# Fused cross-attention and routed feed-forward: last quad and tail reordered, one weight load of the first quad a step later

## The chip, the cores and the metric

The kernel runs on one core of a Trainium2 chip. The metric is device time in microseconds (us). The engines are TensorE (PE, matrix products; PEld is its weight load), VectorE (DVE), ScalarE (ACT), GpSimd (POOL) and SyncE (SP), whose queue starts all transfers here. Each engine works through its own list of instructions in order and waits on semaphores.

## What is computed

Eight batches of 128 rows with 512 columns go through a cross-attention layer (32 query heads, 4 key and value heads, 256 keys: 128 context rows and the 128 rows themselves), then through a feed-forward layer with one matrix of signs, whose input and output channels are scaled by a softmax routing over 8 experts. Both have a layer norm ahead and a residual sum behind.

```python
q = (latents @ Wq).reshape(b, q_len, N_KV_HEADS, N_GROUPS, HEAD_DIM)
scores = jnp.einsum('bqhgd,bkhd->bhgqk', q, k) * scale
attn = jax.nn.softmax(scores.astype(jnp.float32), axis=-1)
out = jnp.einsum('bhgqk,bkhd->bqhgd', attn, v)
x = x + out.reshape(b, q_len, N_HEADS * HEAD_DIM) @ Wo
# feed-forward, on xf = layernorm(x)
routing = jax.nn.softmax(xf @ gate_w.T, axis=1)
in_scale = routing @ in_channel_scale
out_scale = routing @ out_channel_scale
x = x + (xf * in_scale @ sign(weight).T * out_scale + bias)
```

## The kernel before

Everything is float32 in accuracy: each operand of a matrix product is split into a high part (`HI`, rounded) and a low part (`LO`, the rest), and a product is the sum of high by high, high by low and low by high. ScalarE makes the high parts (`o_half`, `p_half`, `z_half`, `wo_half`), VectorE or POOL the low ones (`o_rest`, `z_rest`; POOL's `p_rest`, `wo_rest`).

A prologue (to about 134 us) projects values, keys and the first queries. Then come 8 quads: four groups g of 8 query heads, each in two quads of 4 heads. A quad has 8 steps t, one for each batch. In step t TensorE does, in this order, `attend` (probabilities by values into `av_bank`), `scores` of the batch three steps ahead (`LEAD = 3`), a piece of the next quad's queries (`q_product`), and `project_out`, 12 products into `wo_bank`. The probabilities go from VectorE's 32x32 turns through a round trip in memory: SyncE writes them (`park_p`) and fetches them a step later as `p_low` (`fetch_p`); ScalarE copies them to `p_high` (`p_half`), and POOL leaves the rest in `p_low`. VectorE scales the sums in `av_bank` (`o_scale`), ScalarE copies the high half to `oT`, VectorE the low half.

The query products work on differences and sums of weight blocks (a scheme of seven products): SyncE loads raw blocks R11, R21, R22, R12 (`load_block`), in steps 2 to 5 for the quad after the next, behind waits on POOL's difference (`sum_ready`) and remainders (`wq_lo`). All of SyncE's transfers stand in one list, so `fetch_p` of the next step waits behind `load_block`.

In the last quad (g = 3, qd = 1) there are no next queries. From t = 1 on `final_step(t)` weaves in the feed-forward part of earlier batches: `ffn_stats(t - 1)` (VectorE: mean and variance), `ffn_norm(t - 1)` (ScalarE: `yf`), `y_transpose(t - 1)` (TensorE, into `router_bank`), `yt_copy`, and then for t - 2 `logits`, `gate_max`, `gate_exp`, `gate_route`, `route_transpose`, `routet_copy`, `channel_scales`, and for t - 3 `z_make`, `z_half`, `z_rest`, `ffn_product`, `ffn_scale`. POOL computes 1/sqrt of the variance (`make_rstd`), adds the bias (`bias_add`) and the scaled product (`ffn_add`), after which SyncE stores the batch. Behind step 7 each engine has a list written out by hand, the tail, which finishes batches 4 to 7; batch 7 is done in two halves by `last_product` and `last_out`. `router_bank` alternates between the two banks of `t_bank`.

## Time and profile before

| what | us |
|---|---|
| runs, lowest / median / highest of 3 | 667.48 / 668.85 / 671.62 |
| the profiled execution | 668.46 |
| its span, first to last instruction | 666.6 |
| TensorE busy in the span | 651.5 (98%) |
| VectorE / ScalarE / POOL busy | 483.7 / 376.2 / 397.1 |
| mean granted TensorE clock | 0.997 |

The profile is of one execution. A row of a timeline gives the start, the length, the engine, the line of the kernel, the operation, output and inputs, and in brackets the idle time before it with the engine and line that released it. Rows of several like instructions in sequence carry their number (x12), and the length is from the first's start to the last's modelled end; a following row may begin up to some 0.25 us before that end, as products overlap.

### The profile page before, as it was taken

To read this page: it belongs to the slowest core of one execution; us is meant where nothing else is said; L and a number is where in the kernel's file an instruction comes from. 1 tells how busy PE (TensorE), PEld (TensorE's weight loads), DVE (VectorE), ACT (ScalarE), POOL (GpSimd) and SP (SyncE) were. 2 spreads that over 40 slices of the span, in tenths; PEclk is the share of its full clock that TensorE was granted. 3 is DMA by queue.
4 is the path that set the end of the run, shared out by engine and by line. 5 is a ranking of instruction groups with operands and counts; after the bars stand their busy time and mean duration, and the time that the engine had idled before them with its cause. 6 is when DMAs were issued, how large, how long until landed. Compare 5 with 4: busy or idle time off the path is not lost.

```text
span 666.6 us, 11046 instructions
## 1 busy us (share of the span) xinstructions
PE 651.5 (98%) x3292; PEld 548.1 (82%) x3292; DVE 483.7 (73%) x915; ACT 376.2 (56%) x925; POOL 397.1 (60%) x315
## 2 busy tenths in 40 slices
PE   6999999999999999999999999999999999999997
PEld 4888888888788888888888888888888888877875
DVE  5553232578797889788878887888888788978765
ACT  3335242665576557555764675567556755666543
POOL 3226755275577547645854595467547759955585
PEclk9999999999999999999999999999999999999998
DMA  8575675476888898788878888887888787876502
GB/s 316 206 252 184 248 257 200 144 239 221 280 284 260 256 263 284 257 258 269 276 249 260 270 287 256 267 266 261 257 264 273 257 275 260 289 233 222 185 36 81
DMA packets 96476, 161.68 MB, mean 243 GB/s; under 512 B 9064, under 2 KB 49256, under 8 KB 95392
## 3 DMA queue, kind: packets, MB, share of 16 engines
q1 hardware_dynamic: 96416, 160.97, 73.5%
q8 instruction: 27, 0.44, 0.3%
q14 instruction: 33, 0.27, 0.1%
HBM read 108.38 MB, written 52.56 MB: 241 GB/s over the span
## 4 chain that ended last, share of the span: by engine, by line
PE 89%; DVE 3%; DMA 2%; ACT 2%; POOL 2%; issue 1%; SPq 0%; DVEq 0%; ACTq 0%; POOLq 0%
PE bank L1501 27%; PE bank L1659 25%; PE bank L1605 20%; PE bank L1644 12%; PE bank L1737 2%; DMA p_low<-p_park 1%; ACT prob L886 1%; DMA p_park<-p_turned 1%; DMA raw_a<-in_L_xattn_Wv 1%; POOL p_low L618 1%; PE bank L1694 1%; PE bank L1709 1%; PE bank L1510 1%; PE bank L1686 1%; DVE bank L1270 0%
## 5 line engine op out<-in xcount | busy, mean ns | idle before, releaser
L618 POOL TENSOR_TENSOR p_low<-p_low,p_high 128x1024 fp32r<-128x1024 f32 x64 | 153.8, 2402 | 162.1 <-ACT p_high L760 161.9
L1659 PE MATMUL bank<-wo_pair,oT 128*128 128x512 f32 x768 | 188.2, 392 | 3.0 <-DVE oT L1092 3.0
L1659 PEld LDWEIGHTS bank<-wo_pair,oT 128*128 128x128 f32 x768 | 139.7, 188 | 29.8 <-issue 3.4
L886 ACT ACTIVATE prob<-bank,nmax 128x256 f32<-128x256 f32 x256 | 118.9, 470 | 68.3 <-DVE nmax L1236 63.2
L1501 PEld LDWEIGHTS bank<-kg,qT 128*128 128x128 f32 x768 | 107.8, 190 | 9.9 <-issue 0.2
L1236 DVE TENSOR_REDUCE nmax<-bank 128x2 f32<-128x512 f32 x128 | 87.2, 684 | 37.4 <-PE bank L1501 36.8
L1501 PE MATMUL bank<-kg,qT 128*128 128x256 f32 x768 | 111.2, 282 | 0.0
L1256 DVE STREAM_TRANSPOSE p_turned<-prob 128x512 f32<-128x512 f32 x128 | 90.1, 705 | 28.9 <-ACT prob L886 23.1
L760 ACT ACTIVATE oT<-bank 128x512 fp32r<-128x512 f32 x64 | 38.3, 598 | 112.7 <-DVE bank L1270 112.7
L1605 PE MATMUL bank<-xT,wq_ring 128*128 128x512 f32 x336 | 82.5, 391 | 0.6 <-DVE qT L1169 0.6
L648 POOL TENSOR_TENSOR wq_ring<-raw_a,wq_ring 128x512 fp32r<-128x512 f32 x42 | 54.5, 1297 | 28.0 <-ACT wq_ring L760 28.0
L1605 PEld LDWEIGHTS bank<-xT,wq_ring 128*128 128x128 f32 x336 | 60.7, 188 | 11.5 <-issue 0.8
L760 ACT ACTIVATE p_high<-p_low 128x1024 fp32r<-128x1024 f32 x64 | 67.6, 1057 | 3.1 <-DMA p_low<-p_park 2.8
L1644 PE MATMUL bank<-p_high,vg 128*128 128x512 f32 x256 | 68.7, 390 | 0.0
L1605 PE MATMUL bank<-x_sum,wq_ring 128*128 128x512 f32 x252 | 62.0, 395 | 0.0
L1644 PEld LDWEIGHTS bank<-p_high,vg 128*128 128x128 f32 x256 | 48.0, 188 | 9.8
L1605 PEld LDWEIGHTS bank<-x_sum,wq_ring 128*128 128x128 f32 x252 | 45.9, 188 | 9.4
L886 ACT ACTIVATION_READ_ACCUMULATOR prob<-bank,nmax 128x1 f32 x256 | 50.6, 197 | 0.0
L1092 DVE TENSOR_TENSOR oT<-bank,oT 128x512 fp32r<-128x512 f32 x64 | 44.2, 691 | 2.2 <-ACT oT L760 1.0
L1263 DVE TENSOR_TENSOR acc<-bank,acc 128x512 f32<-128x512 f32 x64 | 43.1, 674 | 2.6 <-PE bank L1659 2.6
L654 POOL TENSOR_TENSOR wo_pair<-raw_b,wo_pair 128x512 fp32r<-128x512 f32 x32 | 40.4, 1302 | 1.9 <-ACT wo_pair L760 1.8
L1644 PE MATMUL bank<-p_low,vg 128*128 128x512 f32 x128 | 39.7, 391 | 1.1 <-POOL p_low L618 1.1
(135 smaller groups left out, 913.4 us busy)
## 6 DMA issues: line engine op xcount, KB each, us to landing
p_park<-p_turned SPq DMA_DIRECT2D x64, 512.0 KB, 3.7
p_low<-p_park SPq DMA_DIRECT2D x64, 512.0 KB, 5.9
kg<-k_park SPq DMA_DIRECT2D x64, 256.0 KB, 3.0
vg<-v_park SPq DMA_DIRECT2D x64, 256.0 KB, 3.8
v_park<-v_stage SPq DMA_DIRECT2D x8, 1024.0 KB, 4.4
raw_a<-in_L_xattn_Wq SPq DMA_DIRECT2D x32, 256.0 KB, 5.4
raw_b<-in_L_xattn_Wo SPq DMA_DIRECT2D x32, 256.0 KB, 5.4
k_park<-k_stage SPq DMA_DIRECT2D x8, 1024.0 KB, 4.6
```

The lines of the kernel that those rows point to most:

```text
L618: nc.gpsimd.tensor_tensor(part, part.bitcast(fp32), p_high[:, :].rearrange("p i c q -> p (i c q)"), ALU.subtract).then_inc(p_lo, 1)
L648: nc.gpsimd.tensor_tensor(slot[:, LO], q_left[u], slot[:, HI], ALU.subtract).then_inc(wq_lo, 1)
L760: return nc.scalar.activation(dst, src, ACT.Copy)
L886: ins = nc.scalar.activation(prob[:, p, j], s_bank[p][:, j * KEYS:(j + 1) * KEYS], ACT.Exp, bias=nmax[:, p, j:j + 1], accum_out=esum[:, t ...
L1092: return nc.vector.tensor_tensor(dst, a, b, ALU.subtract)
L1236: nc.vector.tensor_reduce(nmax[:, p], s_bank[p][:, :].rearrange("p (h k) -> p h k", h=2), AX.X, ALU.max, negate=True).then_inc(max_ready[p ...
L1256: nc.vector.transpose(turned_place(j)[:, :, 2 * p:2 * p + 2, :].rearrange("p k h q -> p h k q"), prob[:, p].rearrange("p h (k e) -> p h k ...
L1263: nc.vector.tensor_tensor(acc[:, t], wo_bank[:, :], acc[:, t], ALU.add).then_inc(acc_ready, 1)
L1501: last = nc.tensor.matmul(dst, left(a, c), right(b, c), start=(n == 0), stop=(n == 3 * chunks - 1))
L1605: last = nc.tensor.matmul((x_bank if piled else proj_bank)[h][:, :], left[:, a, c, h * P:(h + 1) * P], right[:, b, c, :], start=(n == 0), ...
L1644: last = nc.tensor.matmul(av_bank[:, :], vg[:, j % 2, vs, kc, :], ps[:, :, kc, :], start=(n == 0), stop=(n == 3 * KC - 1))
L1659: last = nc.tensor.matmul(wo_bank[:, :], oT[:, s, h, :], wo_pair[:, w, h, :], start=((s, w) == TERMS[0] and h == 0), stop=((s, w) == TERMS ...
```

## The change

1. First quad: `load_block(2, R11)` moves from step 2 to step 3, next to `load_block(2, R21)`; TensorE's first product of the second quad no longer waits for all low query parts.
2. Last quad: half of the projection (two heads) is done by `project_first`: high `oT` by both weight parts for both heads, then low `oT`. It waits for the low half of `oT`, and for a high or low weight part, only where that is used.
3. Steps 2 and 7 of the last quad: routing stands ahead of statistics and norm on VectorE and ScalarE (`LATE_NORM`), and in steps 1, 2 and 7 the y transposes stand behind the whole projection (`LATE_ROWS`). In step 2 ScalarE's `p_half` comes ahead of `o_half`.
4. Tail: another order on TensorE, VectorE and ScalarE. Batch 7 has a bank of its own for its routing (`s_bank[1]` in place of `t_bank[1]`), and the first half of its last product takes `t_bank[1]`. POOL's list is unchanged.

```diff
-        router_bank = t_bank * (B // 2)
+        router_bank = (t_bank * (B // 2))[0:B - 1] + [s_bank[1]]
-        last_prod = [s_bank[1], av_bank]
+        last_prod = [t_bank[1], av_bank]
...
+        LATE_NORM = (2, B - 1)
+        LATE_ROWS = (1, 2, B - 1)
...
-                    if t in (2, 3, 4, 5) and not last:
+                    if t in (2, 3, 4, 5) and not last and (q, t) != (0, 2):
                         sp.wait_ge(wq_lo, split(q + 1, {2: 2, 3: 3, 4: 4, 5: 6}[t]))
                         sp.wait_ge(sum_ready, summed(q + 1, 3))
+                        if (q, t) == (0, 3):
+                            load_block(q + 2, R11)
                         load_block(q + 2, (R11, R21, R22, R12)[t - 2])
...
@@ ScalarE, final_step @@
-                early = 1 < t < B - LEAD
+                early = 2 < t < B - LEAD
                 if early:
                     ffn_norm(t - 1)
+                if t == 2:
+                    p_half(g, qd, t + 1)
                 o_half(g, qd, t)
...
+                if t == 2:
+                    exps(g, qd, t + LEAD, 0)
+                if t in LATE_NORM:
+                    routet_copy(t - 2)
                 if not early:
                     ffn_norm(t - 1)
...
@@ VectorE, tail @@
             accumulate(G - 1, QUADS - 1, B - 1)
+            ffn_stats(B - 1)
             z_make(B - 3)
-            ffn_stats(B - 1)
             gate_max(B - 2)
             z_rest(B - 3)
             gate_route(B - 2)
-            ffn_scale(B - 4)
             gate_factor(B - 2)
             gate_max(B - 1)
             z_make(B - 2)
             gate_route(B - 1)
+            ffn_scale(B - 4)
+            gate_factor(B - 1)
             z_rest(B - 2)
-            gate_factor(B - 1)
+            z_make(B - 1)
             ffn_scale(B - 3)
-            z_make(B - 1)
             z_rest(B - 1)
...
@@ TensorE @@
                     if u == 0:
-                        pe.wait_ge(proj_lo, queries(q - 1, h + 5) if q > 1 else queries(0, UNITS))
+                        if q > 1:
+                            pe.wait_ge(proj_lo, queries(q - 1, h + 5))
...
+            def project_first(g, qd, t, heads):
+                pe.wait_ge(acc_ready, steps(g, qd, t))
+                pe.wait_ge(o_hi, steps(g, qd, t + 1))
+                for h in heads:
+                    for w in (HI, LO):
+                        if t == 0 and w == LO:
+                            pe.wait_ge(wo_lo, count(g, QH, qd, h + 1))
+                        elif t == 0:
+                            pe.wait_ge(wo_hi, count(g, QH, qd, h + 1))
+                        nc.tensor.matmul(wo_bank[:, :], oT[:, HI, h, :], wo_pair[:, w, h, :],
+                                         start=(w == HI and h == heads[0]), stop=False)
+                pe.wait_ge(o_lo, steps(g, qd, t + 1))
+                for h in heads:
+                    last = nc.tensor.matmul(wo_bank[:, :], oT[:, LO, h, :], wo_pair[:, HI, h, :],
+                                            start=False, stop=False)
...
```

How the instructions move is best seen in the engines' lists. TensorE around the projection of step 2 of the last quad, before (`ident,yf` is the y transpose, `ident,route` the routing transpose, `routeT,scales` and `scales,routeT` the channel scales):

```order
L1659 MATMUL bank<-wo_pair,oT 128x512 [waits o_lo,o_hi,acc_ready]
L1659 MATMUL bank<-wo_pair,oT 128x512 x5
L1701 MATMUL bank<-ident,route 128x128 [waits route_ready]
L1686 MATMUL bank<-ident,yf 128x128 [waits y_ready]
L1686 MATMUL bank<-ident,yf 128x128 x3
L1659 MATMUL bank<-wo_pair,oT 128x512 x6
L1709 MATMUL bank<-routeT,scales 128x128 [waits routet_copied]
L1709 MATMUL bank<-routeT,scales 128x128 x3
L1717 MATMUL bank<-scales,routeT 128x512 [waits sgnt_copied]
```

and the same place in the changed kernel:

```order
L1680 MATMUL bank<-wo_pair,oT 128x512 [waits o_hi,acc_ready]
L1680 MATMUL bank<-wo_pair,oT 128x512 x3
L1684 MATMUL bank<-wo_pair,oT 128x512 [waits o_lo]
L1684 MATMUL bank<-wo_pair,oT 128x512
L1743 MATMUL bank<-ident,route 128x128 [waits route_ready]
L1699 MATMUL bank<-wo_pair,oT 128x512 x6
L1751 MATMUL bank<-routeT,scales 128x128 [waits routet_copied]
L1751 MATMUL bank<-routeT,scales 128x128 x3
L1759 MATMUL bank<-scales,routeT 128x512 [waits sgnt_copied]
L1728 MATMUL bank<-ident,yf 128x128 [waits y_ready]
L1728 MATMUL bank<-ident,yf 128x128 x3
```

The wait for the low half moved behind four products, and the y transposes behind the channel scales.

VectorE in the same step, before, from the addition of the projection (L1263) over the scaling of `av_bank` (L1270) to the second maximum:

```order
L1263 TENSOR_TENSOR acc<-bank,acc 128x512 [waits wo_ready]
L1095 BN_STATS stats<-acc 128x6 [waits acc_ready]
L1097 BN_AGGR mv<-stats 128x2 [waits stats_ready]
L1270 TENSOR_TENSOR bank<-bank,r_all 128x512 [waits r_in0,av_ready]
L1301 TENSOR_REDUCE bank<-bank 128x1 [waits logit_ready]
L1307 TENSOR_SCALAR gbias<-bank,rstd 128x1 [waits rstd_ready,gmin_ready]
L1092 TENSOR_TENSOR oT<-bank,oT 128x512 [waits o_hi]
L1236 TENSOR_REDUCE nmax<-bank 128x2 [waits s_ready0]
L1316 TENSOR_SCALAR route<-bank 128x2x8 [waits gexp_ready]
L1319 TENSOR_REDUCE gsum<-bank 128x1
L1092 TENSOR_TENSOR route<-bank,route 128x8 [waits route_hi]
L1236 TENSOR_REDUCE nmax<-bank 128x2 [waits s_ready1]
```

and changed:

```order
L1278 TENSOR_TENSOR acc<-bank,acc 128x512 [waits wo_ready]
L1285 TENSOR_TENSOR bank<-bank,r_all 128x512 [waits r_in0,av_ready]
L1316 TENSOR_REDUCE bank<-bank 128x1 [waits logit_ready]
L1322 TENSOR_SCALAR gbias<-bank,rstd 128x1 [waits rstd_ready,gmin_ready]
L1107 TENSOR_TENSOR oT<-bank,oT 128x512 [waits o_hi]
L1331 TENSOR_SCALAR route<-bank 128x2x8 [waits gexp_ready]
L1334 TENSOR_REDUCE gsum<-bank 128x1
L1107 TENSOR_TENSOR route<-bank,route 128x8 [waits route_hi]
L1251 TENSOR_REDUCE nmax<-bank 128x2 [waits s_ready0]
L1110 BN_STATS stats<-acc 128x6 [waits acc_ready]
L1112 BN_AGGR mv<-stats 128x2 [waits stats_ready]
L1251 TENSOR_REDUCE nmax<-bank 128x2 [waits s_ready1]
```

The statistics moved from ahead of the scaling to behind the routing and the first maximum.

TensorE in the tail, before, from the high products of batch 5 (`z_pair`) to the last routing transpose:

```order
L1737 MATMUL bank<-wq_ring,z_pair 128x512 [waits z_hi,acc_ready]
L1737 MATMUL bank<-wq_ring,z_pair 128x512 x3
L1686 MATMUL bank<-ident,yf 128x128 [waits z_lo,y_ready]
L1686 MATMUL bank<-ident,yf 128x128 x3
L1701 MATMUL bank<-ident,route 128x128 [waits route_ready]
L1737 MATMUL bank<-wq_ring,z_pair 128x512 [waits z_lo]
L1737 MATMUL bank<-wq_ring,z_pair 128x512 x3
L1694 MATMUL bank<-gateT,yT 128x8 [waits yt_copied]
L1694 MATMUL bank<-gateT,yT 128x8 x3
```

and changed, from the y transposes of batch 7, which now stand first:

```order
L1728 MATMUL bank<-ident,yf 128x128 [waits exp_ready1,y_ready]
L1728 MATMUL bank<-ident,yf 128x128 x3
L1779 MATMUL bank<-wq_ring,z_pair 128x512 [waits z_hi,acc_ready]
L1779 MATMUL bank<-wq_ring,z_pair 128x512 x3
L1743 MATMUL bank<-ident,route 128x128 [waits route_ready]
L1736 MATMUL bank<-gateT,yT 128x8 [waits yt_copied]
L1736 MATMUL bank<-gateT,yT 128x8 x3
```

The y transposes no longer wait for `z_lo`, and the last logits (`gateT,yT`) stand directly behind the routing transpose; the four low products of batch 5 come later.

## Rows read from the trace of the kernel before

**Rows 1.** Stretches: from:to, length, busy PE, PEld, DVE, ACT, POOL, PEclk, DMA share, GB/s
```profile
134.00:171.00 37.00, 35.33 (x179) 29.55 (x178) 27.23 (x51) 21.43 (x54) 25.96 (x17) 1.00 0.76 244
171.00:582.00 411.00, 411.00 (x2096) 350.51 (x2095) 338.08 (x612) 254.36 (x656) 258.36 (x157) 1.00 0.83 266
582.00:597.80 15.80, 14.82 (x90) 12.45 (x88) 11.54 (x22) 10.95 (x28) 10.65 (x11) 1.00 0.75 246
597.80:605.40 7.60, 6.03 (x37) 4.90 (x37) 6.07 (x19) 4.96 (x14) 1.86 (x1) 1.00 0.76 241
605.40:641.00 35.60, 35.60 (x201) 30.16 (x200) 27.85 (x74) 21.01 (x48) 22.75 (x31) 1.00 0.49 164
641.00:649.30 8.30, 7.68 (x42) 6.05 (x41) 5.40 (x15) 3.65 (x7) 7.41 (x14) 1.00 0.08 32
649.30:663.20 13.90, 12.73 (x69) 10.39 (x67) 9.28 (x27) 5.79 (x12) 9.04 (x12) 0.88 0.16 60
```
**Rows 2.** The same view of half-microsecond stretches around the clock's fall
```profile
656.50:657.00 0.50, 0.13 (x2) 0.02 (x1) 0.37 (x1) 0.44 (x3) 0.50 (x1) 0.82 0.00 0
657.00:657.50 0.50, 0.50 (x3) 0.50 (x3) 0.46 (x3) 0.50 (x1) 0.50 (x1) 0.50 0.00 0
...
660.00:660.50 0.50, 0.50 (x3) 0.36 (x3) 0.50 (x1) 0.36 (x1) 0.00 (x0) 0.76 0.00 0
```
**Rows 3.** First quad: timeline of TensorE and ScalarE, and a wait of SyncE
```profile
136.29 2.97 PE L1605 MATMUL bank<-xT,wq_ring 128*128 128x512 f32 x12 [0.61 <-DVE qT L1169]
...
SPq L484 <- POOL raw_a L642: 5.4, 1, 5.4
...
166.00 1.06 ACT L760 ACTIVATE p_high<-p_low 128x1024 fp32r<-128x1024 f32 x1 [2.83 <-DMA p_low<-p_park]
...
169.57 0.73 PE L1644 MATMUL bank<-p_low,vg 128*128 128x512 f32 x2 [1.05 <-POOL p_low L618]
```
**Rows 4.** Timeline of step 0 of the last quad, POOL and TensorE
```profile
581.36 5.03 POOL L654 TENSOR_TENSOR wo_pair<-raw_b,wo_pair 128x512 fp32r<-128x512 f32 x4 [0.19 <-ACT wo_pair L760]
...
584.54 3.00 PE L1659 MATMUL bank<-wo_pair,oT 128*128 128x512 f32 x12 [0.98 <-DVE oT L1092]
```
**Rows 5.** Timeline of step 2, all engines, and the landing times of p_low
```profile
591.72 0.37 SPq L431 DMA_DIRECT2D p_low<-p_park  x1
...
597.78 1.68 PE L1501 MATMUL bank<-kg,qT 128*128 128x256 f32 x12
...
597.98 0.70 DVE L1095 BATCH_NORM_STATS2 stats<-acc 128x6 f32<-128x512 f32 x1
...
598.81 0.68 DVE L1270 TENSOR_TENSOR bank<-bank,r_all 128x512 f32<-128x512 f32 x1
...
599.56 0.58 ACT L760 ACTIVATE oT<-bank 128x512 fp32r<-128x512 f32 x1
...
601.00 1.62 PE L1659 MATMUL bank<-wo_pair,oT 128*128 128x512 f32 x6 [1.54 <-DVE oT L1092]
...
DMA to landing us min/median/max: 3.8/5.9/7.8
```
**Rows 6.** Timeline of step 3, VectorE and TensorE
```profile
608.25 0.68 DVE L1092 TENSOR_TENSOR z_pair<-bank,z_pair 128x512 fp32r<-128x512 f32 x1
...
609.08 2.03 PE L1737 MATMUL bank<-wq_ring,z_pair 128*128 128x512 f32 x8
```
**Rows 7.** Timeline of step 7 and the tail, ScalarE, TensorE, POOL and VectorE
```profile
643.38 0.60 ACT L760 ACTIVATE oT<-bank 128x512 fp32r<-128x512 f32 x1 [0.54 <-DVE bank L1270]
...
644.84 1.63 PE L1659 MATMUL bank<-wo_pair,oT 128*128 128x512 f32 x6 [0.48 <-DVE oT L1092]
...
656.29 0.33 PE L1701 MATMUL bank<-ident,route 128*128 128x128 f32 x1 [0.77 <-DVE route L1092]
...
662.09 1.28 POOL L611 TENSOR_TENSOR acc<-acc,oscale 128x512 f32<-128x512 f32 x1 [2.19 <-DVE oscale L1335]
...
664.00 0.42 DVE L1348 TENSOR_TENSOR acc<-bank,acc 128x256 f32<-128x256 f32 x1
```

More of the change, by code:

```diff
@@ L1043, in final_step @@
                     exps(g, qd, t + LEAD, 1)
-                if t >= 2:
+                if t >= 2 and t not in LATE_NORM:
                     routet_copy(t - 2)
@@ L1745, in last_product @@
                 half = D // 2
-                pe.wait_ge(exp_ready[1], steps(G - 1, QUADS - 1, B))
+                pe.wait_ge(z_lo, B - 2)
                 for s in (HI, LO):
```

51 lines of the change are left out of this document (34 added, 17 removed).

## The prediction

> **What bounds the kernel now.** I read the stretches first, because they show where TensorE, the engine that is busy 98% of the time, is not busy. In [rows 1] the second column is the length of a stretch, the third TensorE's busy time, and PEclk the granted clock. From 171 to 582 us TensorE is busy 411.00 of 411.00 us, and again 35.60 of 35.60 between 605.4 and 641. What a faster order can win is therefore the rest: 37.00 - 35.33 = 1.67 us in the first quad, 15.80 - 14.82 = 0.98 in steps 0 and 1 of the last quad, 7.60 - 6.03 = 1.57 in its step 2, 8.30 - 7.68 = 0.62 in step 7, and 13.90 - 12.73 = 1.17 in the tail. The tail also runs at a mean clock of 0.88, so 13.90 x 0.12 = 1.67 us of its full-speed work time is lost. [rows 2] shows when: the clock leaves 1.00 (2.4 GHz) at about 656.8, stands at 0.50 (1.2 GHz) from 657 and is back after 660. Together that is 7.7 us, and no reordering of this kind can give more before the last product. A second limit stands behind it, the additions, output transfers and their completion up to 666.6. I then read each of these waits in the timeline, engine by engine.
>
> **First quad.** Two TensorE waits stand there [rows 3]. The first, 0.61 us, is on VectorE's qT: the first product of the next queries waits for all low query parts of the old ones. The change drops this wait for the first quad; what is left is a wait on its own left operand, made long before. TensorE then arrives 0.6 us earlier at everything that follows; POOL's and ScalarE's work of these steps hangs on scores that come earlier with it, and no further wait of TensorE stands before 169.57, so I keep the whole 0.6. The second, 1.05 us, is on POOL's p_low. It is late from far off: SyncE stands 5.4 us before the load of a raw weight block, waiting for POOL's difference of two blocks, and the fetch of the next p_low is queued behind it; ScalarE's p_high then waits 2.83 us for that transfer. The change moves this load one step on, behind the fetch and next to a load that has the same two waits. The fetch goes out up to 5.4 us earlier, lands before ScalarE is free for it, and 1.05 us falls away. The moved load costs one more issue in step 3 and is wanted two steps later, so I price it at nothing; if it did delay the fetch of step 5, that fetch has the 5.4 us gained before it. First quad: 0.6 + 1.05 = 1.65 us. Both ends: nothing (the waits return one product later) and 1.67, all of the stretch. I take 1.65, since in the following 411 us nothing outruns TensorE's work [rows 1].
>
> **Step 0 of the last quad.** The order of the output projection becomes: four high products of two heads, which need only ScalarE's high half, then their two low ones, then the other heads. TensorE now waits 0.98 us for VectorE's low half [rows 4]. But in this step the low weights are late too: POOL makes them in 5.03 us from 581.36, so the fourth head's is ready at 586.39. A product takes (3.00 - 1.62) / 6 = 0.23 us, by the rows of twelve and of six [rows 4, 5], and that head's begin nine products after 584.54, at 586.6. Starting earlier can only bring this to 586.4. So of 0.98 us I count 0.2. In step 1 the y transposes move behind the rest of the projection and no longer stand in for ScalarE's yf: 0.2 to 0.3. For both steps I take 0.5.
>
> **Step 2.** The largest single wait is here, 1.54 us before 601.00 [rows 5]. The row of VectorE's statistics (597.98, 0.70 us, and 0.18 behind it) stands ahead of the scaling at 598.81, and ScalarE takes oT at 599.56. The change puts statistics behind the routing and the first maximum, so that the scaling comes 0.8 us earlier, and lets TensorE start on the high half, which now lies ready 0.86 us before TensorE starts (599.56 + 0.58 = 600.14 against 601.00). Together 1.66, more than the wait, so TensorE goes on right after the scores (597.78 + 1.68 = 599.46). The added risk is on ScalarE: p_high of the next step now stands in front of oT, and needs its transfer. That is issued at 591.72 and lands, at the median of 5.9 us, at 597.6; scaling and oT's turn come at about 598.5, and the copy of 1.06 us (the length of ScalarE's row in [rows 3]) ends just there. Behind it the routing (route, exp, routeT) goes ahead of yf, and the y transposes go behind the channel scales; by my layout each comes within 0.1 us of TensorE. Step 3 then starts 2.1 us earlier: 0.5 of steps 0 and 1, 1.5 of this wait, and 0.1 of smaller ones.
>
> **Given back in steps 3 and 4.** VectorE does not come 2.1 us earlier. Its statistics are only put later in the same step, and its chain through exp and the turns gains some 0.65 us. TensorE's low feed-forward products need z_pair, ready at 608.25 + 0.68 = 608.93, and start four products after 609.08, at 610.0 [rows 6]. That slack of 1.1 plus 0.65 is 1.75 against 2.1, so 0.35 to 0.4 us comes back as a wait, and another 0.1 at routeT. I carry 1.6 us from step 3 on. Steps 5 and 6 keep their old order and follow TensorE, so they keep it.
>
> **Step 7 and the tail.** In step 7 TensorE waits for oT (0.48 by its row, 0.62 with what lies around it [rows 1, 7]); the high half is there at 643.38 + 0.60 = 643.98 and TensorE free at 644.84 - 0.62 = 644.22, so all of it goes, and the routing in front of the statistics keeps the rest level: 0.65. In the tail the last logits move in front of four low products, and the last y transposes get a bank of their own, so they no longer stand behind z_lo. The last routing, now ending at 656.2 just before its transpose at 656.29, comes 0.65 + 0.9 (four products) + 0.3 (the bank) = 1.9 us earlier, 654.3. I find products to put under each wait, save three of 0.1 to 0.35 us. If the clock does not fall, TensorE's last product ends 0.65 + 1.17 + 1.67 less 0.2 = 3.3 us earlier.
> That is not the end of the kernel. POOL's five additions of 1.28 us now begin only after the scaling of batch 4, which the change puts behind the last routing: 654.3 + 0.7 + 5 x 1.28 = 661.4, against 662.09 + 1.28 = 663.4 now. VectorE's last addition, now 664.00 + 0.42 = 664.4, comes at about 661.0. So POOL's chain ends last. Behind VectorE's last addition the span now runs on for 666.6 - 664.4 = 2.2 us; behind POOL's, two more transfers have to be issued first, at 0.37 us (the length of SyncE's row in [rows 5]). 661.4 + 0.7 + 2.2 = 664.3 against 666.6: a gain of 2.3 for step 7 and tail together.
>
> **The clock in the sum.** Just before the fall TensorE had waited 0.77 us [rows 2, 7]. The much longer wait before 601.00 [rows 5] left the clock at 1.00 [rows 1], so the sum is of both. In the changed tail the waits are shorter, so I take the fall as gone. If it stays, TensorE ends 1.67 later; POOL's chain hides 0.4 of it, leaving 1.2 to 1.3. The Trainium skill (TensorE: Matmul & The Clock Gate, Part 4: PE-mode transpose) says that transposes do not count as PE-busy in the way matmuls do. By that the fall would stay, since the tail keeps all its transposes; the trace cannot separate that from the waits.
>
> **Sum.** 1.65 + 1.6 + 2.3 = 5.55 us. The profiled execution took 668.46 us (span 666.6), so it would take 662.9. The median of the runs is 668.85, 0.4 above; I give 663.2.
>
> **The rivals.**
> 1. Forecast, 661.9 to 664.2: chance 0.50.
> 2. Waits replaced or clock still falling: 0.30. If p_low of step 2 lands after 7.8 us, the longest in the trace [rows 5], oT is held until 600.5 and 1 to 1.5 us of step 2 is lost; or the tail's fall stays and costs 1.25; or the first quad's 1.65 comes back as another wait. One of them gives 664.4 to 664.9, two 666. Of the 0.30 the fall has 0.12, p_low 0.08, the first quad 0.05, two of them 0.05. For it: these waits sit on chains over four engines, with 0.1 us to spare at several places. Against it: the median landing of 5.9 leaves no gap.
> 3. POOL does not end last, because its additions overlap other than laid out, or steps 3 and 4 give nothing back: 3.3 in place of 2.3, or 2.1 in place of 1.6. Then 661.7 to 662.2: 0.16.
> 4. Slower than before: the clock falls early, in step 7, and stays down. Behind the first six projection products (644.84 + 1.63 = 646.5) 2.8 us of work is left in it [rows 7], and 12.73 - 1.67 = 11 in the tail. Each microsecond of that work at half speed costs one more, so it decides once more than 5.6 us of it runs slow; over 1% slower needs 12. All 14 slow would give 663.2 + 14 = 677. Step 7 already has its waits and the clock is 1.00 through it [rows 1]: 0.04.
>
> **How the numbers follow.** About 1% is what a measurement of this kernel can tell from no change. 1% below 668.85 is 662.2, inside the forecast's lower edge: 0.08 of its 0.50 lies there, and 0.16 of rival 3: faster 0.24. Rival 4 gives slower 0.03. Same 0.73. The range leaves out rival 4, the worst of rival 2 and the best of rival 3: 661.2 to 666.4.
>
> **What would show it.** First quad: TensorE's waits on qT near 136 and p_low near 169 gone, stretch 134 to 171 shorter by 1.6. Step 0: still some 0.7 us idle, now for wo_lo in the fourth head. Step 2: no TensorE wait over 0.3, a new one before z_pair in step 3. Tail: clock 1.00 until the last product; the last compute instruction POOL's addition. I am wrong if ScalarE's p_high holds oT in step 2, if the clock still falls, or if VectorE's halves end last.

## The result and the profile after

| kernel | runs | median us | lowest to highest |
|---|---|---|---|
| before, in this comparison | 6 | 670.02 | 667.48 to 672.67 |
| changed | 6 | 663.48 | 662.88 to 666.28 |

The ratio of changed to before is 0.9925, with a 95% interval from 0.9897 to 0.9953. The two medians of the table lie further apart, 6.5 us; with six runs each and a spread of 5 us in those of before, the ratio is the safer figure. Taken on 668.5, about the median of before in the later comparisons, that is 5.0 us (3.1 to 6.9). The kernel is faster, by somewhat less than 1%. A second comparison of the same two kernels (e9 below) gave 0.9941 [0.9923, 0.996], 3.9 us. The profiled execution of the changed kernel took 664.52 us with a span of 662.7, against 668.46 and 666.6.

The stretches, cut at the same events as [rows 1]:

```profile
133.88:171.00 37.12, 37.12 (x189) 31.38 (x188) 28.59 (x53) 23.28 (x58) 26.77 (x17) 1.00 0.79 259
171.00:580.57 409.57, 409.57 (x2089) 349.11 (x2087) 337.07 (x609) 252.90 (x653) 258.55 (x157) 1.00 0.82 265
580.57:596.40 15.83, 15.03 (x90) 12.36 (x88) 11.48 (x22) 11.00 (x28) 10.73 (x11) 1.00 0.79 253
596.40:602.70 6.30, 5.64 (x36) 4.84 (x36) 4.91 (x15) 4.25 (x12) 3.72 (x5) 1.00 0.76 249
602.70:638.80 36.10, 36.10 (x204) 30.13 (x203) 28.66 (x76) 21.75 (x51) 21.02 (x26) 1.00 0.53 169
638.80:646.60 7.80, 7.78 (x41) 5.68 (x39) 6.13 (x16) 3.70 (x7) 6.54 (x14) 1.00 0.09 34
646.60:658.30 11.70, 11.13 (x69) 9.19 (x68) 8.70 (x27) 5.74 (x12) 8.85 (x12) 1.00 0.13 48
```

The first quad has no idle time any more (37.12 of 37.12; before 35.33 of 37.00), and step 7 none (7.78 of 7.80). The tail stands at a clock of 1.00 (before 0.88) and has 0.57 us idle. What is left is in steps 0 to 2: 0.80 and 0.66 us. TensorE's waits over the whole kernel behind the prologue, in the view of waits (engine, line, what was waited for, total, times, longest):

```profile
PE bank L1680 <- ACT oT L769: 0.7, 1, 0.7
PE bank L1680 <- issue: 0.4, 1, 0.4
PE bank L1793 <- ACT z_pair L769: 0.3, 1, 0.3
PE bank L1699 <- POOL wo_pair L663: 0.2, 1, 0.2
PE bank L1736 <- ACT yT L769: 0.2, 1, 0.2
```

Of the waits of before, qT, p_low, the last route and the last routeT are gone ([rows 3, 7]), and 3.0 us on VectorE's oT have become 0.7 us on ScalarE's oT. The places of that one and of the kernel's end, in the timeline (rows answering [rows 5, 7]):

```profile
596.47 0.69 DVE L1285 TENSOR_TENSOR bank<-bank,r_all 128x512 f32<-128x512 f32 x1
...
597.04 1.06 ACT L769 ACTIVATE p_high<-p_low 128x1024 fp32r<-128x1024 f32 x1 [1.62 <-DMA p_low<-p_park]
598.00 0.58 ACT L769 ACTIVATE oT<-bank 128x512 fp32r<-128x512 f32 x1
...
598.72 1.16 PE L1680 MATMUL bank<-wo_pair,oT 128*128 128x512 f32 x4 [0.66 <-ACT oT L769]
...
653.20 1.30 POOL L620 TENSOR_TENSOR acc<-acc,oscale 128x512 f32<-128x512 f32 x1 [2.41 <-DVE route L1107]
...
656.04 2.11 PE L1793 MATMUL bank<-wq_ring,z_pair 128*128 128x256 f32 x16 [0.29 <-ACT z_pair L769]
...
656.94 2.54 POOL L620 TENSOR_TENSOR acc<-acc,oscale 128x512 f32<-128x512 f32 x2
...
658.99 0.42 DVE L1363 TENSOR_TENSOR acc<-bank,acc 128x256 f32<-128x256 f32 x1
```

VectorE had scaled the sums at 597.16, but ScalarE waited 1.62 us for the transfer that p_high needs, and oT stood behind it. At the end POOL's addition is the last compute instruction (656.94 + 2.54 = 659.48), 0.07 us behind VectorE's (659.41).

In the first quad the fetch of p_low that went out at 160.09 before, and whose copy waited 2.83 us [rows 3], now goes out 5.7 us earlier, and its copy has no wait:

```profile
154.41 0.37 SPq L437 DMA_DIRECT2D p_low<-p_park  x1
...
162.84 1.06 ACT L769 ACTIVATE p_high<-p_low 128x1024 fp32r<-128x1024 f32 x1
```

One table holds what nine of the profiles say of the places in question, in us between starts of the same rows (e4 and the four with an added delay are taken up with their runs). First quad: from TensorE's first row of step 0 to that of step 5. "Tail": from the logits of batch 6 to the last product. "End": from the last product to the end of the span.

| profile of | first quad | last quad, steps 0 to 3 | step 2 alone | step 7 | tail | end |
|---|---|---|---|---|---|---|
| before | 43.77 | 34.35 | 9.91 | 8.26 | 11.85 | 5.48 |
| changed | 41.66 | 33.50 | 9.05 | 7.83 | 9.43 | 6.66 |
| changed, again (e9) | 42.72 | 32.62 | 8.25 | 7.83 | 9.43 | 6.67 |
| e1, first quad alone | 41.81 | 34.44 | 9.90 | 8.26 | 10.66 | 5.71 |
| e2, steps of the last quad alone | 41.53 | 32.63 | 8.26 | 7.83 | 11.74 | 5.42 |
| e3, tail alone | 41.77 | 34.31 | 9.90 | 8.27 | 9.76 | 6.63 |
| e7, before with filler | 41.56 | 34.37 | 9.90 | 8.27 | 10.64 | 5.69 |
| e8, changed, scaling early | 41.80 | 32.59 | 8.27 | 7.83 | 9.45 | 5.77 |
| e10, e8 and oT first | 41.61 | 33.50 | 8.73 | 7.83 | 9.43 | 5.77 |

The gain of the profiled pair is so 2.1 (first quad) + 0.85 (steps 0 to 3) + 1.67 (step 7, tail and end together) = 4.6 us; 0.5 was lost ahead of step 0, in the prologue that the change doesn't touch (its end lay between 132.89 and 134.08 in the profiles without an added delay), and 0.2 in the six quads between. That makes 3.9, the difference of the spans.

Those six quads are not quite the same in every profile. From step 5 of the first quad to the start of the last, TensorE took 403.50 us in the profile of before and 403.67 in that of the changed kernel, and between 403.50 and 404.84 in all. The three lowest, 403.50 (before and e5) and 403.53 (e9), are those of the executions with a wait of TensorE in the first quad; the eleven without one have 403.60 to 404.84. So some of what the first quad gains can be lost behind it. I had taken it as kept, since TensorE was busy in all of the 411 us [rows 1].

### The profile page after: what moved, and what is told of

It reads as the page before. It is cut to its first block, busy times and chain, and to the rows that moved or that the text cites. A ratio compares the mean times of both kernels' runs of the same rounds, so it can differ in the third digit from the quotient of the medians.

```text
span 662.7 us, 11042 instructions
## 1 busy us (share of the span) xinstructions
PE 650.5 (98%) x3292; PEld 546.4 (82%) x3292; DVE 483.6 (73%) x915; ACT 376.3 (57%) x925; POOL 397.7 (60%) x315
## 4 chain that ended last, share of the span: by engine, by line
PE 92%; DMA 2%; issue 1%; SPq 1%; DVE 1%; ACT 1%; POOL 0%; POOLq 0%; DVEq 0%; ACTq 0%
PE bank L1520 30%; PE bank L1699 24%; PE bank L1625 20%; PE bank L1664 12%; PE bank L1779 2%; DMA p_low<-p_park 1%; PE bank L1680 1%; PE bank L1736 1%; DMA raw_a<-in_L_xattn_Wv 1%; DMA r_all<-r_park 1%; PE bank L1529 1%; PE bank L1728 0%; SPq L429 0%; PE bank L1751 0%; PE bank L1684 0%
## 5 line engine op out<-in xcount | busy, mean ns | idle before, releaser
L1699 PE MATMUL bank<-wo_pair,oT 128*128 128x512 f32 x720 | 175.8, 392 | 0.2 <-POOL wo_pair L663 0.2
L1699 PEld LDWEIGHTS bank<-wo_pair,oT 128*128 128x128 f32 x720 | 131.1, 188 | 25.1 <-POOL wo_pair L663 0.6
```

The lines of the kernel that those rows point to most:

```text
L1699: last = nc.tensor.matmul(wo_bank[:, :], oT[:, s, h, :], wo_pair[:, w, h, :], start=((s, w) == TERMS[0] and h == 0), stop=((s, w) == TERMS ...
```

## The experiments

Each was compared with the kernel before on the same chip. Ratios carry their 95% intervals.

| kernel | median us | before there | ratio |
|---|---|---|---|
| e1, first quad alone | 667.84 | 668.51 | 0.9981 [0.9967, 0.9996] |
| e2, steps alone | 665.26 | 668.51 | 0.9960 [0.9941, 0.9979] |
| e3, tail alone | 667.06 | 668.51 | 0.9985 [0.9968, 1.0002] |
| e4, changed, oT ahead of p_high | 663.70 | 668.51 | 0.9928 [0.9904, 0.9952] |
| e5, before, two transfers late | 670.29 | 668.03 | 1.0026 [1.001, 1.0042] |
| e6, e1, two transfers late | 667.40 | 668.03 | 0.9984 [0.9969, 1.0] |
| e7, before with filler | 667.15 | 668.03 | 0.9977 [0.9953, 1.0002] |
| e8, changed, scaling early | 662.65 | 668.03 | 0.9906 [0.9889, 0.9923] |
| e9, changed, again | 664.42 | 668.58 | 0.9941 [0.9923, 0.996] |
| e10, e8 and oT first | 663.57 | 668.58 | 0.9927 [0.9903, 0.9952] |
| e11, changed, p_low of step 2 late | 665.77 | 668.58 | 0.9965 [0.9942, 0.9988] |
| e12, e11 with oT first | 664.78 | 668.58 | 0.9945 [0.9924, 0.9965] |

**e1, the first quad's edits alone** (the load of R11 a step later, and the wait of the first product dropped).

```diff
-                    if t in (2, 3, 4, 5) and not last:
+                    if t in (2, 3, 4, 5) and not last and (q, t) != (0, 2):
...
-                        pe.wait_ge(proj_lo, queries(q - 1, h + 5) if q > 1 else queries(0, UNITS))
+                        if q > 1:
+                            pe.wait_ge(proj_lo, queries(q - 1, h + 5))
```

> Only the first quad's two edits, on the kernel before. Between the starts of attend in steps 0 and 5 of the first quad the kernel before takes 43.77 us, the changed one 41.66. Theory (both waits fall away and nothing takes their place): 41.7 here too, and the 2.1 us reach the end of the span: time 2 us (0.3%) below the kernel before, last quad as before it, clock falling in the tail as before. Rival (the waits come back further on, where VectorE or SyncE are late): attend of the last quad starts less than 1 us earlier, time unchanged.

By the ratio 0.19%, or 1.3 us. The quad took 41.81 us against 43.77. But e2 and e3, which have the old first quad, took 41.53 and 41.77. So the two waits that I had priced at 1.65 are not always there. The tail, which e1 leaves as it was, took 10.66 and not 11.85: the clock had not fallen in this execution. The edit of the qT wait shows by itself here: VectorE waited 4.46 us for its park write, longer than the 4.11 of before, and TensorE had no wait on qT.

**e2, the steps of the last quad alone**

```diff
-                project_out(g, qd, t, (0, 1))
+                project_first(g, qd, t, (0, 1))
...
+                if t == 2:
+                    p_half(g, qd, t + 1)
                 o_half(g, qd, t)
```

(and with them all of part 3 of the change.)

> Only the changes inside the last quad's steps (high products first, routing ahead of statistics, y transposes late), with the old first quad and the old tail. Theory (VectorE's z_pair gives part back): step 2 is 0.9 us shorter, step 3 0.4 longer, step 7 0.4 shorter, together 1.2 us from step 0 to the tail's start; the tail, old, keeps its length, so the time is 1.2 us (0.2%) lower. Rival (steps and tail only help together, because the old tail waits for statistics that are now later): 0.5 us or less.

The largest part: 0.40%, 2.7 us, more than twice the 1.2 us that I expected. Its step 2 took 8.26 us, not 9.05. ScalarE's rows, to be read beside those of the changed kernel above:

```profile
590.66 0.37 SPq L436 DMA_DIRECT2D p_low<-p_park  x1
...
595.65 1.06 ACT L765 ACTIVATE p_high<-p_low 128x1024 fp32r<-128x1024 f32 x1 [0.47 <-DMA p_low<-p_park]
596.96 0.60 ACT L765 ACTIVATE oT<-bank 128x512 fp32r<-128x512 f32 x1 [0.24 <-DVE bank L1281]
```

The same fetch landed 5.0 us after its issue, oT waited for VectorE and not for p_high, and TensorE had no wait on oT. Two rows tell why the first quad was also short in e2 with its old order: VectorE's turn behind the park write, and ScalarE's copy of p_low.

```profile
132.36 1.30 DVE L1267 STREAM_TRANSPOSE p_turned<-prob 128x512 f32<-128x512 f32 x2 [3.12 <-DMA p_park<-p_turned]
...
163.49 1.06 ACT L765 ACTIVATE p_high<-p_low 128x1024 fp32r<-128x1024 f32 x1 [1.19 <-DMA p_low<-p_park]
```

In the profile of before the turn had waited 4.1 us and the copy started at 166.00 [rows 3]. Both transfers simply came earlier here: the fetch for that copy went out at 159.23 and was used 4.3 us later, where in the profile of before 5.9 us lay between the two (160.09 to 166.00). In e3 and e7, with the same order, it was 4.5 and 4.4 us.

**e3, the tail and the bank alone**

```diff
-            ffn_product(B - 3, (LO,))
             logits(B - 1)
             channel_scales(B - 2)
+            ffn_product(B - 3, (LO,))
```

(and the rest of part 4 of the change.)

> Only the tail's order and the bank of its own for batch 7, with old steps and old first quad. Theory (waits and clock are cured by the tail's own order): from the tail's start to the last product's start 9.4 to 9.7 us instead of 11.85, clock 1.00 throughout, POOL's last addition ends at or after VectorE's, so the span shrinks by only 1.2 to 1.5 us. Rival (the clock fell by its own rule, transposes not counting as activity, whatever the order): the clock falls to 0.50 again somewhere in the tail and the last product starts at most 0.9 us earlier.

0.15%, 1.0 us, with an interval that touches no gain. The tail took 9.76 us against 11.85 of before, or 10.66 of e1 without the fall; the stretch behind the last product grew from 5.48 (5.71) to 6.63. From the tail's start to the end of the span: before 17.33, e1 16.37, e3 16.39. Against an execution of the old tail in which the clock stays up, the new one is so worth nothing at the end: TensorE's 0.9 us are given back behind it.

The three parts add up to 0.19 + 0.40 + 0.15 = 0.74%, the whole change gives 0.75% (0.59% in e9). Each of the three intervals reaches 0.15 to 0.19% to either side, so the match rules out a large loss between them and no more.

**e4, the changed kernel with oT ahead of p_high in step 2**

```diff
-                if t == 2:
-                    p_half(g, qd, t + 1)
                 o_half(g, qd, t)
+                if t == 2:
+                    p_half(g, qd, t + 1)
```

> The changed kernel with one swap: in step 2 of the last quad ScalarE copies oT's high half before p_high of the next step. Theory (p_high, waiting for its transfer, holds oT, and that costs 0.66 us of TensorE plus what it costs VectorE): step 2 takes 8.3 to 8.5 instead of 9.05 us; VectorE's low half and all behind it come 0.7 earlier too, so step 3 does not give it back: 0.4 to 0.7 us less than the changed kernel at step 5. Rival (VectorE's chain is the limit either way): step 3 grows by what step 2 loses, and attend of step 5 starts within 0.1 of the changed kernel's.

The ratio is 0.9928, where the changed kernel had 0.9925 and 0.9941: no gain. Its profile says little of the step, since another transfer (VectorE's r_park, 1.94 us of wait) was late in step 1; step 2 took 9.29 us. e10 to e12 took it up again.

**e5 and e6, two transfers made late on purpose**, in the kernel before and in e1. e2 had shown that the waits of the first quad come and go with the landing of two transfers. Here both are held back in every run. The second hold did what it was meant for. The first added little in these profiles: VectorE's wait for the park write was 4.63 us in e5 and 4.31 in e6, within the 2.77 to 5.36 of the profiles without a hold.

```diff
+            def hold(i):
+                sp.dma_start(late_park[i:i + 1, :], x[0, i:i + 1, :]).then_inc(late, 16)
+                sp.wait_ge(late, 16 * (i + 1))
...
+            hold(0)
             park_p(0, 0, 1)
...
+                if q == 0 and t == 3:
+                    hold(1)
                 if not first and not (final and t + 1 >= B):
                     fetch_p(*step_after(g, qd, t, 1))
```

> The kernel before, with two transfers of the first quad made late on purpose: SyncE writes 2 KB to DRAM and waits until they have landed (about 2 us, an estimate from the 2.2 us between the last addition and the end of the span), once ahead of the second park write, once ahead of the fetch of p_low for step 4. Theory A, the two waits of the first quad are an exposure to late transfers: the slack that stood there when they came early (no wait in two profiles of kernels with the old first quad) is used up, and TensorE waits 1 to 3 us at qT and 1 to 3 us at p_low; the kernel is 2 to 5 us slower than before. Theory B, what the edit of the first quad removes is not tied to the landing of transfers: the waits stay at 0.6 and 1.05 or below, and the kernel is within 1 us of before.

> The same two delays in the kernel with only the two edits of the first quad (no wait of the first product for the low query parts; the raw block is loaded a step later). Theory A: the fetch for step 4 has 5.4 us in hand, so the 2 us are hidden there and no wait on p_low stands; the delay of the park write is hidden at the first product and shows at most in part behind it. 2 to 4 us faster than the same delays in the kernel before, against 1.3 us without delays. Rival B: the delays come through another wait (scores, oT or the next query products) and the two delayed kernels differ by less than 1.5 us.

Theory A held, in its mechanism for the fetch above all. In e5 TensorE's rows with a wait in the first quad are these three, and the quad took 45.08 us:

```profile
137.73 3.02 PE L1614 MATMUL bank<-xT,wq_ring 128*128 128x512 f32 x12 [1.15 <-DVE qT L1178]
...
169.46 1.15 PE L1653 MATMUL bank<-p_high,vg 128*128 128x512 f32 x4 [0.37 <-ACT p_high L769]
...
171.83 0.73 PE L1653 MATMUL bank<-p_low,vg 128*128 128x512 f32 x2 [1.21 <-POOL p_low L627]
```

In e6 there is none, although VectorE's turn started at 135.00 (134.80 in e5), and the quad took 41.65. SyncE's rows show where the slack is from; first e5, then e6:

```profile
161.10 0.38 SPq L361 DMA_DIRECT2D raw_a<-in_L_xattn_Wq  x1
161.53 0.52 SPq L417 DMA_DIRECT2D late_park<-in_x  x1
163.84 0.38 SPq L437 DMA_DIRECT2D p_low<-p_park  x1
```

```profile
154.88 0.52 SPq L417 DMA_DIRECT2D late_park<-in_x  x1
158.70 0.38 SPq L437 DMA_DIRECT2D p_low<-p_park  x1
```

With the load moved behind it the fetch went out 5.1 us earlier, in spite of a longer hold. By the medians the delays cost the kernel before 2.3 us, while the one with e1's edits stayed 0.6 below before; the two differ by 2.9 us. So the first quad's edits buy insurance: nothing when the transfers come early, 2.9 us by these medians when they come late, 1.3 us on the mean. Within the first quad the pair of profiles shows more, 3.4 us (45.08 against 41.65), but 1.3 of that is gone again before the last quad: the six quads between took 403.50 us in e5 and 404.84 in e6, where the one wait of TensorE that the profile shows is of 0.32 us on POOL's p_low (at 454.93). So rival B was right in part. What holds TensorE for the rest of the 1.3 us was not traced.

**e7, before with filler under the tail's waits** (four more products, their results unused, so that this kernel has the same waits for the routing but less idle time of TensorE in them).

```diff
+            pe.wait_ge(exp_ready[1], steps(G - 1, QUADS - 1, B))
+            filler(3)
             route_transpose(B - 1)
+            filler(1)
             channel_scales(B - 1)
```

> The kernel before, with four more 128x512 products (results unused) in the tail: three under the wait of 0.77 us in front of the last transpose of the routing, one under the next of 0.37 us. Theory A, the waits bring the clock down: the clock stays 1.00 to the last product, the eight products in front of it take 2.1 us (2.85 before) and the last product starts 1.2 to 1.7 us sooner after the tail's start than the 11.85 us of before, less at most 0.3 for products that don't fit under the waits; by the ratio 0.997 to 1.0, since not all executions had the fall. Theory B, the fall comes from the transposes or from something outside these waits: clock falls to 0.5 as before in profiles of it, and the kernel is equal or up to 0.5 us slower.

The stretch of the tail in e7, and below it that of e2, whose tail is that of before:

```profile
648.57:661.35 12.78, 12.54 (x73) 9.77 (x71) 9.22 (x27) 5.79 (x12) 8.87 (x12) 1.00 0.18 65
```

```profile
645.54:659.30 13.76, 12.61 (x68) 10.61 (x68) 8.91 (x26) 5.87 (x12) 9.76 (x12) 0.88 0.17 60
```

One profile can't settle it, since e1 kept its clock without filler. But every run gives its mean clock. The two profiles with a fall in the tail (before and e2) have 0.997; the other twelve have 0.999 or 1.000, where the clock falls only behind the last product or not at all (in the changed kernel from about 661.4 us on, when all engines are done). I take a mean of 0.997 or less for a fall in the tail, which no run without a trace can confirm. Before had it in 55 of the 84 runs beside these experiments; the four kernels with its tail (e1, e2, e5, e6) in 22 of 40. The kernels with the new tail had it in 1 of 67, and e7 in 0 of 10. So the fall goes with the waits in front of the last routing, and stays away when they are filled or shortened. The filler adds product work as well as it takes idle time away, and no run separates the two. Why the fall comes in some runs with these waits and not in others is open: e1 had both waits, 0.77 and 0.37 us as before, and kept its clock. Among the runs of before those with a fall have medians that lie 0.9, 1.7 and 1.5 us higher on the three chips, but the smaller groups of e1, e2, e5 and e6 scatter between 1.1 lower and 2.4 higher. The tail to the end of the span in e1 is 0.96 us shorter than in before, and 0.8 shorter than in e2.

**e8, the changed kernel with the scaling of batch 4 early.** In the profile after, VectorE stood idle for 1.30 us in front of the last routing while POOL waited for the scaling that stood behind it.

```diff
             gate_factor(B - 2)
+            ffn_scale(B - 4)
             gate_max(B - 1)
             z_make(B - 2)
             gate_route(B - 1)
-            ffn_scale(B - 4)
```

> The changed kernel, with VectorE's scaling of batch 4's product put back between the factor of batch 6 and the maximum of batch 7, where VectorE stood idle for 1.30 us. Theory A, POOL's chain of additions is what ends last: POOL's first addition starts 2 to 2.8 us earlier (650.4 to 651 in place of 653.2), its last ends before VectorE's halves, and the span behind the last product's start shrinks from 6.66 to about 5.5 to 5.8: 0.8 to 1.1 us faster than the changed kernel (0.12 to 0.17%). Theory B, the two transfers at the end are bound by the issue or the completion of the last halves alone: no difference beyond 0.3 us.

POOL and VectorE in e8:

```profile
648.68 0.68 DVE L1350 TENSOR_TENSOR oscale<-bank,oscale 128x512 f32<-128x512 f32 x1
650.09 0.17 DVE L1316 TENSOR_REDUCE bank<-bank 128x1 f32<-128x8 f32 x1 [0.72 <-PE bank L1736]
...
649.78 1.28 POOL L620 TENSOR_TENSOR acc<-acc,oscale 128x512 f32<-128x512 f32 x1
651.03 2.51 POOL L613 TENSOR_TENSOR acc<-acc,bias_b 128x512 f32<-128x512 f32 x2
655.03 2.64 POOL L620 TENSOR_TENSOR acc<-acc,oscale 128x512 f32<-128x512 f32 x2 [1.49 <-DVE oscale L1350]
...
658.08 0.42 DVE L1363 TENSOR_TENSOR acc<-bank,acc 128x256 f32<-128x256 f32 x1
```

POOL's first addition starts 5.35 us ahead of the last product (2.84 before this edit), its last ends at 657.67, 0.8 ahead of VectorE's, and the end shrank from 6.66 to 5.77: the 0.9 us that theory A expected. VectorE's last addition ends 3.37 us behind the start of the last product in both, so it is not what became shorter. SyncE's last two output transfers start 3.85 us behind it in the changed kernel and 2.96 in e8, and the span ends 1.9 us after both are issued in either one. The changed kernel's row, then that of e8:

```profile
659.89 0.90 SPq L519 DMA_DIRECT2D out_y<-acc  x2
```

```profile
658.09 0.93 SPq L519 DMA_DIRECT2D out_y<-acc  x2
```

TensorE's tail stayed at 9.45. e8 has the lowest median of all, of four runs only: 662.65, ratio 0.9906. It ran beside before, not beside the changed kernel; e10, with the same edit and oT first, ran beside e9 and was 0.85 us faster.

**e9, the changed kernel again**

> The changed kernel once more, unchanged, for a second profiled execution and for a direct comparison with the next one. Theory A, what the change gives in step 2 of the last quad hangs on the landing of one p_low fetch (about 5 us after its issue in two kernels whose step took 8.26 us, 5.9 us in the changed kernel's first profile, whose step took 9.05): step 2 takes 8.2 to 9.1 us, and it is 8.3 if ScalarE's wait for that transfer is below 0.6 us. Theory B, step 2 is always 9.0 or more in this kernel for another reason. Time 663 to 664 us; clock 0.998 or more in every run.

Theory A held: ScalarE waited 0.36 us for the transfer, step 2 took 8.25, steps 0 to 3 32.62. The median, 664.42, is 0.4 above the range that I gave. It also shows what the first quad's edits don't cover. VectorE waited longer for the second park write than in any other profile:

```profile
134.90 1.31 DVE L1271 STREAM_TRANSPOSE p_turned<-prob 128x512 f32<-128x512 f32 x2 [5.36 <-DMA p_park<-p_turned]
```

```profile
139.90 2.99 PE L1699 MATMUL bank<-wo_pair,oT 128*128 128x512 f32 x12 [0.47 <-DVE oT L1107]
```

VectorE's scaling and low half stand behind that turn. The quad took 42.72, 1.0 more than the 41.7 of a quad without a wait, of which the profile shows 0.47 as a wait. The same two kernels differ by 5.0 us in one comparison and 3.9 in the other, with intervals that overlap; such landings may be one reason.

**e10, both edits: scaling early and oT first**

> The changed kernel with both edits together: the scaling of batch 4's product put back into VectorE's idle time in the tail, and in step 2 ScalarE's oT ahead of p_high of the next step. Theory A: the tail gives the 0.9 us that it gave alone; in step 2 a late transfer no longer holds oT, and p_high, which TensorE wants only at the start of step 3, still comes in time: 662.4 to 662.9 us, with step 2 at 8.3 to 8.5 whenever the transfer lands. Theory B: oT first costs what it gives, because p_high then ends 0.6 us later and pushes the exp behind it: 662.9 to 664.

The end is 5.77 again. Step 2 took 8.73 us with oT first, against 8.25 to 8.27 in the three profiles with p_high first and a transfer in time: the order of the change is worth 0.5 us when the transfer is punctual. Step 3 gave none of it back (10.11 us against 9.97 to 10.00). With oT first the copy of p_high stands ahead of the routing's exp on ScalarE, which starts 1.44 us behind the start of oT's copy (0.49 in e9), and TensorE's channel scales start 7.59 us into the step (7.21 in e9). This is theory B for that edit; by its median (663.57) the kernel doesn't beat e8.

**e11 and e12, the fetch of step 2 late on purpose**, with p_high first (as changed) and with oT first.

```diff
+                if final and t == 2:
+                    hold(0)
                 if not first and not (final and t + 1 >= B):
                     fetch_p(*step_after(g, qd, t, 1))
```

> The changed kernel, with the p_low fetch of step 2 of the last quad made late on purpose: SyncE writes 2 KB to DRAM and waits for them ahead of it (2.3 to 3.8 us where this was measured). Theory A, oT is held by ScalarE's p_high, which waits for this transfer: ScalarE waits 2.5 to 5 us, oT follows 1.06 us behind the landing, TensorE's wait on oT grows from 0.7 to 2.5 to 4.5 us and the kernel is 2 to 4 us slower than the changed one. Theory B, the 1.6 us wait of ScalarE is not what holds TensorE: TensorE's wait on oT stays below 1.2 and the kernel is within 1 us of the changed one.

> The same delay, with oT ahead of p_high on ScalarE in step 2. Theory A: oT no longer waits for the transfer, p_high is wanted only at the start of step 3 and is there within 0.5 us of it; 1.5 to 3.5 us faster than the same delay with p_high first. Theory B: the delay reaches TensorE anyway at the start of step 3 (p_high, or POOL's p_low behind it) and the two delayed kernels differ by less than 1 us.

First ScalarE and TensorE of e11, then ScalarE of e12:

```profile
594.94 0.38 SPq L443 DMA_DIRECT2D p_low<-p_park  x1
...
598.96 1.06 ACT L777 ACTIVATE p_high<-p_low 128x1024 fp32r<-128x1024 f32 x1 [2.58 <-DMA p_low<-p_park]
599.92 0.58 ACT L777 ACTIVATE oT<-bank 128x512 fp32r<-128x512 f32 x1
...
600.64 1.17 PE L1688 MATMUL bank<-wo_pair,oT 128*128 128x512 f32 x4 [1.62 <-ACT oT L777]
```

```profile
597.13 0.60 ACT L777 ACTIVATE oT<-bank 128x512 fp32r<-128x512 f32 x1 [1.77 <-DVE bank L1293]
597.75 1.06 ACT L777 ACTIVATE p_high<-p_low 128x1024 fp32r<-128x1024 f32 x1
```

The mechanism is shown for p_high first: the longer ScalarE waits for the transfer (0.36, 1.62, 2.58 us), the longer step 2 (8.25, 9.05, 10.02), and with oT first the same delay leaves the step at 8.86. The sizes that I expected were too large: e11 is 1.35 us slower than e9 where I expected 2 to 4, and the two delayed kernels lie 1.0 us apart, which by my own limit (less than 1 us) is as good as theory B. B's path does not show, though: TensorE has no wait at the start of step 3 of e12. The fetch went out 3.75 us later than in e9 but landed only 4.0 us after its issue, where 5.2 were measured there, so TensorE's wait grew to 1.62 and not to 2.5. The intervals of the two overlap; the 1.16 us between the two steps 2 in the traces carry the verdict, one profile each.

## Why the prediction was right, and where it was not

The forecast was 663.2 us with 661.9 to 664.2 for the likeliest case, and 663.48 and 664.42 were measured in the two comparisons. The total came out right with terms that were not: the mean gain is 3.9 to 5.0 us, not the 5.55 of the sum. Taken from the 668.85 that the forecast started from, such a gain gives 663.8 to 664.9, so that the median of 663.48 lies within 0.3 us of 663.2 is luck in part. For the profiled execution, for which the sum was made, it gave 662.9, and 664.52 was measured, outside the likeliest range and inside that of the rival with one failed term (664.4 to 664.9).

The difference of the spans, 3.9 us, follows from the 5.55 by terms: the first quad gave 0.46 more than forecast, steps 0 to 3 0.75 less, step 7 with tail and end 0.63 less, 0.54 went in the prologue and 0.17 in the six quads between. There are two slips in the sums themselves: 668.85 - 5.55 is 663.3, not 663.2, and the second case of rival 3 alone (2.1 in place of 1.6) gives 662.7, not 662.2 or less.

**First quad, forecast 1.65.** In the profiled pair 2.1. The mechanism is as described. The step that failed is that I took both waits from one execution as a fixed price. They were absent in e2, e3 and e7 with the old order. That nothing outruns TensorE in the quads between was taken for granted too, and e6 lost 1.3 us there. The mean worth is about 1.3 us (e1), and it is the worth of an exposure. Rows of before could have told me: the landing times in [rows 5] go from 3.8 to 7.8 us, and a fetch with 5.9 us left TensorE 1.05 us waiting, so one with 4.8 would leave it none. The three without a wait had 4.3 to 4.5.

**Steps 0 and 1, forecast 0.5.** Measured 0.42 (7.56 + 7.30 became 7.56 + 6.88). Step 0 gained nothing of the 0.2 forecast; that POOL's low weights bound it was right, down to the wait of 0.2 us on them in the profile after. All of the gain is in step 1.

**Step 2, forecast 1.5.** 0.86 in the profile after, 1.65 in e2, e8 and e9. This is the rival "p_low late holds oT" (0.08). The step that failed is "the median landing of 5.9 leaves no gap": I left the fetch's issue where it was in before, 3.75 us ahead of the step's start. In the profile after it was 2.55 ahead (591.10 against 593.65), 1.20 less. Step 1 in front of it had become 0.42 shorter, and the issue in front of it took 0.79 us, not 0.37; the rest was not traced. The landing decides with it: in e2 the fetch went out only 2.77 ahead, but landed after 5.0 us instead of 5.9, and ScalarE's wait was 0.47 instead of 1.62. In the profile after the copy ended 0.9 us behind the scaled sums. I had named the condition in absolute times of the old trace, where it has to be counted from the step that moves.

**Given back in step 3, forecast 0.35 to 0.4 and 0.1 in step 4.** Step 3 took 10.01 against 9.58, steps 4 to 6 were equal. So 0.43, the size is right. The reason isn't. I had put it down to TensorE coming 2.1 us earlier than VectorE. In e11 step 2 is no shorter than before and TensorE reaches step 3 only 0.4 us earlier in the quad than before (24.35 against 24.77), yet its step 3 takes 9.99. That points to the new order of step 2 itself: in e11 as in the changed kernel the eight feed-forward products of step 3 take 2.22 instead of 2.03 us, waiting inside for z_pair, and VectorE's row for it stands 4.1 us behind the step's start, where it stood 2.9 behind it before ([rows 6], with the step's start at 605.38). These products are 0.2 of the 0.43. Which of the moved rows does it was not tried.

**Step 7, forecast 0.65.** 0.43 in each of the profiles with the new steps. I had counted the wait by the stretch's idle time of 0.62; the new order gives 0.2 of it back.

**Tail and end.** TensorE's last product comes 2.42 us earlier within the tail, 1.19 of it from the clock (before against e1) and 1.2 from the order; I had 1.17 + 1.67 - 0.2 = 2.64. That POOL's chain would end last was right, at 659.48, where the forecast of 661.4 less the 2.23 us by which step 7 starts earlier (638.78 against 641.01) gives 659.2, and e8 shows it: with the chain out of the way the end is 0.9 us shorter. Step 7, tail and end together gave 1.67 against 2.3 forecast. What was mis-sized is the clock. I priced the fall at 1.67 of work and 1.2 at the end and took it as certain. It costs 0.96 at the end of the span (e1 against before), which is 0.29 of the missing 0.63; 0.22 is step 7, and 0.12 what is left of the tail. The fall also comes in only about two runs of three, so that the tail's mean worth is near 0.6 us by these two numbers and 1.0 by e3's ratio.

**The clock and transposes.** By the mean clock of the runs the old tail had the fall in 77 of 124. The new tail holds the same transposes and products in another order and had it in 1 of 67. The Trainium skill (TensorE: Matmul & The Clock Gate, Part 4: PE-mode transpose) says that transposes don't count as busy in the same way; a fall in spite of closer rows, which I had drawn from it as a rival, did not come in any profile of the new tail. The same page (section: Why this matters for your kernels) advises against long idle gaps, since they bring the clock down. The longest wait near this fall is 0.77 us [rows 7], and one of 1.54 us at another place [rows 5] left the clock at 1.00, so here the length of the longest gap does not tell where it falls. The measurement decides; what else about the stretch matters is open.

**The slower rival** (a fall in step 7) did not occur: the clock is 1.00 through it in the profile after.

## What to carry to other kernels

A wait that ends with a transfer is not a constant: before pricing its removal, take the landing times of that transfer over the whole trace and ask at which of them the wait begins. When a reorder puts an instruction that needs a transfer in front of one that doesn't, count the time from the transfer's issue to its use in the new schedule, in which the steps before it may have become shorter. And when the busiest engine finishes earlier, look at once at what ends last behind it: here one scaling of 0.7 us, put back into a gap of VectorE, gave 0.9 us in the profiles, about what the whole new order of the tail gave alone (1.0, with an interval that reaches no gain).

## What the runs showed of the hardware that I had not expected

- Landing times of one and the same fetch of 512 KB (p_low for step 3 of the last quad) counted from issue to use: 4.0 us in e11, 5.0 in e2, 5.2 in e9, 5.4 in e8, 5.9 in the changed kernel's first profile. VectorE's wait for one park write near 130 us was between 2.77 and 5.36 us in the profiles of the kernels without an added delay, which are the same up to there. Single runs of the kernel before lie between 665.7 and 672.7; how much of this spread such landings make up was not measured.
- The mean granted clock was 0.997 or less in 55 of 84 runs of the same program and 1.000 in the rest.
- A 2 KB transfer to memory and the wait for it held SyncE for 2.3 us (161.53 to 163.84, e5) in one place and 3.8 us (154.88 to 158.70, e6) in another.
